# A deformable convolution on one core: one of 18 sampled columns in three of four rows made by TensorE from an image in SBUF instead of gathered

## What is computed

```
offsets = conv(x_group).reshape(B, H, W, 9, 2)
loc = clip(grid + kernel_grid + offsets, 0, 127)          # x, y
wa = (x1 - x) * (y1 - y); wb = (x1 - x) * (y - y0)
wc = (x - x0) * (y1 - y); wd = (x - x0) * (y - y0)
sampled = wa * img[y0, x0] + wb * img[y1, x0] + wc * img[y0, x1] + wd * img[y1, x1]
s = pointwise(depthwise3x3(sampled))
```

## Time and profile before

| | |
|---|---|
| timed executions | 12,372.78, 12,374.86 and 12,376.20 us, median 12,374.86 |
| span of the profiled execution, first to last instruction | 17,350.5 us |
| POOL, 9,216 gathers | busy 8,708.9 us, 945 ns each |
| DVE busy | 5,165.4 us |
| PE busy | 8,037.3 us |
| granted TensorE clock, mean | 0.694 |

### The profile page before, as it was taken

How to read it: one execution, slowest core, us unless ns; L and a number is a source line. 1 busy time by engine, 2 the same in 40 slices (tenths; PEclk the granted TensorE clock), 3 DMA queues, 4 the chain that set the end, 5 groups by cost and what they waited for, 6 DMA issues and landing times.

```text
span 17350.5 us, 102336 instructions
## 1 busy us (share of the span) xinstructions
PE 8037.3 (46%) x30934; PEld 5581.5 (32%) x30934; DVE 5165.4 (30%) x5993; ACT 1769.5 (10%) x2822; POOL 8759.5 (50%) x9300
## 2 busy tenths in 40 slices
PE   4444444445345544443335555344325555443358
PEld 2223223223234432232224443232223443222245
DVE  2222222322333233233222233223223223222323
ACT  1001101110000011100000001110000001110014
POOL 4555555455554555455554455555555444545530
PEclk7667677667667776666667777666667777666679
DMA  2222222222223321222123321222112332122233
GB/s 78 68 60 66 78 62 70 72 61 77 61 75 98 98 60 48 63 80 59 43 61 99 98 84 45 57 77 68 46 52 77 98 98 61 48 64 77 60 124 118
DMA packets 878203, 1254.74 MB, mean 72 GB/s; under 512 B 183384, under 2 KB 663064, under 8 KB 859992
## 3 DMA queue, kind: packets, MB, share of 16 engines
q0 software_dynamic: 294912, 604.57, 13.7%
q1 hardware_dynamic: 511784, 596.71, 10.7%
q10 hardware_dynamic: 71344, 51.39, 0.9%
HBM read 1069.42 MB, written 245.43 MB: 76 GB/s over the span
## 4 chain that ended last, share of the span: by engine, by line
another core or an unknown queue 40%; PE 20%; issue 19%; DVE 10%; ACT 3%; PEldq 2%; PEld 1%; SPq 1%; DMA 1%; ACTq 1%; DVEq 1%
PE acc L1307 8%; PE stage L1163 6%; DVE srow L1685 5%; PE stage L1035 2%; PEldq L483 2%; DVE gathered L1678 2%; PE pt L1294 1%; ACT stt L1008 1%; PEld acc L1307 1%; PE stage L1102 1%; PE stage L1081 1%; DMA off<-offs 1%; DVE wtn L1647 0%; SPq L694 0%
## 5 line engine op out<-in xcount | busy, mean ns | idle before, releaser
L543 POOL DMA_INDIRECT gathered<-table,idx x9216 | 8708.9, 945 | 7844.0 <-issue 4412.7
L1307 PE MATMUL acc<-stt,room 128*128 128x256 f32 (+2 forms) x15360 | 4368.5, 438 | 4763.0 <-ACT stt L1008 2491.7
L1307 PEld LDWEIGHTS acc<-stt,room 128*128 128x128 f32 (+1 forms) x15360 | 3242.4, 221 | 5803.8 <-issue 2728.6
L1685 DVE TENSOR_REDUCE srow<-gathered 128x576 f32<-128x2304 f32 x512 | 2097.1, 4096 | 324.7 <-remote 207.2
L1163 PE MATMUL stage<-room 128*128 128x128 f32 x6784 | 1035.3, 303 | 1067.5 <-issue 1049.5
L1163 PEld LDWEIGHTS stage<-room 128*128 128x128 f32 x6784 | 962.5, 218 | 1139.8 <-issue 1134.0
L1678 DVE TENSOR_TENSOR gathered<-gathered,wtb 128x2304 f32<-128x2304 f32 x512 | 1304.4, 2548 | 1.2 <-issue 1.2
L1008 ACT ACTIVATE stt<-pt 128x1024 f32<-128x1024 f32 (+1 forms) x512 | 415.6, 812 | 8375.5 <-remote 4988.2
L1666 DVE SCALAR_TENSOR_TENSOR xs<-acc,fused,xr 128x256 f32<-128x256 f32 x128 | 61.7, 482 | 3747.9 <-PE acc L1307 2206.0
L1035 PE MATMUL stage<-room,mat 128*128 128x512 f32 (+1 forms) x1360 | 776.2, 694 | 841.1 <-issue 338.9
L1294 PE MATMUL pt<-mat,srow 128*128 128x128 f32 x2048 | 427.2, 337 | 1475.6 <-DVE srow L1685 1250.7
(11 more groups left out here) (212 smaller groups left out, 4575.2 us busy)
## 6 DMA issues: line engine op xcount, KB each, us to landing
gathered<-table,idx POOLq DMA_INDIRECT x9216
room<-toep SPq DMA_DIRECT2D x48, 1792.0 KB, 7.0
room<-toep SPq DMA_DIRECT2D x64, 1280.0 KB, 8.0
room<-toep SPq DMA_DIRECT2D x64, 768.0 KB
table<-room SPq DMA_DIRECT2D x64, 512.0 KB
toep<-in_taps SPq DMA_DIRECT2D x128, 224.0 KB
gathered<-toep SPq DMA_DIRECT2D x16, 1792.0 KB, 7.0
toep<-in_taps SPq DMA_DIRECT2D x128, 160.0 KB
```

Source lines behind the costliest of these rows:

```text
L543: nc.gpsimd.indirect_dma_start(gat[r][:, k % K9 * G + k // K9, :], None, table[b].rearrange("(n e) -> n e", e=PAIR), bass.IndirectOffsetOn ...
L1307: ins = nc.tensor.matmul(sums_of[:, pairs, :], wk[0:kk, m, dx, at:at + P], stt[0:kk, slots, m, dx:dx + W], start=start and m == 0 and dx == 0,
L1685: nc.vector.tensor_reduce(srow[r % 2][:].rearrange("p (s c) -> p s c", c=CG), gat[r][:].rearrange("p s (q c) -> p s c q", q=4), AX.X, ALU. ...
```

## The change

In rows 0, 1 and 2 of each step the last column (k = 17: group 1, the tap at the lower right) is no longer gathered; POOL issues 17 indirect DMAs for these rows and 18 for row 3. The sampled values of this column are made by other engines.

Group 1's 32 channels of the whole image lie in SBUF, x on the partitions, then y, then channel (`image`, two buffers, filled by ACT's queue in one DMA for each image). Interpolation in x is a product with a matrix of "hat" weights max(0, 1 - |x - xpos|), 128 x 128 for each row (`hat_x`). PE multiplies it by the image in eight **pieces** of four channels x 128 y (`dense_piece`), alternately into the banks `acc[1]` and `pt`. DVE multiplies each piece in PSUM by hat weights in y (`hat_y`) and sums over y into four values of `srow` (`dense_column`). The hats are made once for a step (`hats`), from positions that SP's queue writes to HBM (`xrow`) and loads again to all partitions (`load_columns`); the index chain has four operations more.

```diff
+DENSE = 3
+DK = GK - 1
+PIECES = CG // 4
+        def dense_bank(j):
+            return (acc[1][:] if j % 2 == 0 else pt[:].rearrange("p a w -> p (a w)")).rearrange("p (c y) -> p c y", c=4)
...
-                        for k in range(GK):
+                        for k in range(gathered_of(r)):
                             nc.gpsimd.indirect_dma_start(
...
                         sp.wait_ge(off_used, n + 1)
                         load_offsets(n + 1, nb, ni)
+                        sp.wait_ge(hat_made, n + 1)
+                        load_columns(nb, ni)
...
+                def load_image(b):
+                    act.dma_start(image[b % 2], pixels(b)).then_inc(img_in, 16)
...
+                def dense_done(n, r):
+                    pe.wait_ge(dense_summed, PIECES * (DENSE * n + r) + PIECES + 2)
...
+                def dense_piece(n, b, r, j):
+                    pe.wait_ge(dense_summed, PIECES * (DENSE * n + r) + j + 1)
+                    nc.tensor.matmul(dense_bank(j), hat_x[:, r, :], image[b % 2][:, :, 4 * j:4 * j + 4].rearrange("x y c -> x c y"),
+                                     start=True, stop=True).then_inc(dense_p, 1)
...
                         turn_full(v, r)
-                        yield 3 * r + 3
+                        if r < DENSE:
+                            yield 3 * r + 2.1
...
+                            dense_piece(n, b, r, 0)
...
-                            products(r, slots, pairs, full[:1], start=r == 1 and not first)
+                            for j in range(6):
+                                products(r, slots, pairs, (j // 3,), start=r == 1 and not first, dxs=(j % 3,))
+                                if r < DENSE:
+                                    dense_piece(n, b, r, j + 2)
+                            if r < DENSE:
+                                yield 3 * r + 3
+                            products(r, slots, pairs, full[2:3], dxs=(0, 1))
+                            if r < DENSE:
+                                dense_done(n, r)
+                            products(r, slots, pairs, full[2:3], dxs=(2,))
                             turn_rest(r)
...
+                def hats(n):
+                    at_x = base0[:, 0, 2:3]
+                    ts(hat_x, xpos, at_x, None, ALU.subtract)
...
+                def dense_column(n, r):
+                    if r == 0:
+                        dve.wait_ge(hat_made, n + 1)
+                    for j in range(PIECES):
+                        k = PIECES * (DENSE * n + r) + j + 1
+                        dve.wait_ge(dense_p, k)
+                        at_y = hat_y[:, r:r + 1, :].to_broadcast([P, 4, H])
+                        tt(dense_bank(j), dense_bank(j), at_y, ALU.mult).then_inc(dense_weighted, 1)
+                        dve.wait_ge(dense_weighted, k)
+                        c = DK * CG + 4 * j
+                        nc.vector.tensor_reduce(srow[r % 2][:, c:c + 4], dense_bank(j), AX.X, ALU.add).then_inc(dense_summed, 1)
...
+                        if r < DENSE:
+                            yield 3 * r + 2.1
+                            dense_column(n, r)
+                        if r == ROWS - 1 and not last:
+                            hats(n + 1)
```

More of the change, by code:

```diff
@@ L298, in in_pairs @@
             return [pair + twice(*shape) for pair in first]
+        image = twice(H, CG)
+        ramp, y_far = carve(W + 1), carve(ROWS)
+        xpos, hat_y = several(2, DENSE, W)
+        hat_x = gathered[:, 0:DENSE, GK - 1, :]
+        spare = image[1].rearrange("p y c -> p (y c)")
+        cw0 = spare[:, 0:12 * C].rearrange("p (k c) -> p k c", c=C)
+        offw = spare[:, 12 * C:12 * C + 12 * NOFF].rearrange("p (k o) -> p k o", o=2 * NOFF)
         at[0] = 0
@@ L782, in _ @@
                 meet = meeting(sp)
-                for a in (*bands_out, offs_out, x2_out, *cx_out, *mix_out, *abg_out, *s_out, *res_out, *table_out):
+                for a in (*bands_out, offs_out, xrow_out, x2_out, *cx_out, *mix_out, *abg_out, *s_out, *res_out, *table_out):
                     sp.sem_inc(a, 1)
@@ L1018, in _ @@
                 act.sem_inc(right_entries, 2)
-                drive(act, meet, step, lambda: None, {"modulate": ln_and_exp, "close": ln_and_exp},
+                drive(act, meet, step, lambda: load_image(0), {"modulate": ln_and_exp, "close": ln_and_exp},
                       {"conv_norm": norm, "shift": shift, "conv_shift": lower_part, "table_norm": norm,
@@ L1299, in turn_rest, with products @@
                         .then_inc(turned, 1)
-                def products(r, slots, pairs, chunks, start=False):
+                def dense_piece(n, b, r, j):
+                    pe.wait_ge(dense_summed, PIECES * (DENSE * n + r) + j + 1)
+                    nc.tensor.matmul(dense_bank(j), hat_x[:, r, :], image[b % 2][:, :, 4 * j:4 * j + 4].rearrange("x y c -> x c y"),
+                                     start=True, stop=True).then_inc(dense_p, 1)
+                def products(r, slots, pairs, chunks, start=False, dxs=range(3)):
                     at = BLOCK_AT[r] * C
@@ L1305, in products @@
                         kk = P if m < MCH - 1 else C
-                        for dx in range(3):
+                        for dx in dxs:
                             ins = nc.tensor.matmul(sums_of[:, pairs, :], wk[0:kk, m, dx, at:at + P],
@@ L1318, in step @@
                         turn_full(v, r)
-                        yield 3 * r + 3
+                        if r < DENSE:
+                            yield 3 * r + 2.1
+                            if r == 0:
+                                if first:
+                                    pe.wait_ge(img_in, 16 * (b + 1))
+                                pe.wait_ge(hat_made, n + 1)
+                            dense_piece(n, b, r, 0)
+                        else:
+                            yield 3 * r + 3
                         pe.wait_ge(full_ready, v + 1)
@@ L1327, in step @@
                         if r == 0 and isinstance(n, int) and n == 0:
+                            for j in range(1, PIECES):
+                                dense_piece(n, b, r, j)
+                            yield 3 * r + 3
+                            dense_done(n, r)
                             turn_rest(r)
@@ L1636, in indices @@
                     then(ts(loc[:], loc[:], 0.0, float(W - 1), ALU.max, ALU.min))
+                    y_of = xy(loc, 1)[:, :, DK]
+                    then(stt_(y_far, y_of, float(W - 1), y_of, ALU.is_ge, ALU.add))
                     then(nc.vector.tensor_copy(inti, loc[:]))
@@ L1696, in first_index @@
                     indices(0)
+                    hats(0)
                 def start():
```

86 lines of the change are left out of this document (69 added, 17 removed).

## The result

The changed kernel takes **14,971.26 us** (median of 4 runs, 14,968.94 to 14,972.43); the kernel before took 12,374.35 beside it. The ratio is **1.2098 [1.2081, 1.2115]**: 21% slower. I had said 14,200, between 12,900 and 15,300. The direction, the mechanism and the price of a piece were as forecast; the forecast is 760 us short, one claim on the profile was wrong, and another is shown only in part.

What follows compares the result with a forecast made beforehand. POOL's gathers bound the kernel before, 89.9 us a step; afterwards DVE and PE in lockstep would. 128 x 90.9 = 11,635, + 1,375 + 290 + 100 + 188 + 620 gave 14,210, said as 14,200 us (+15%), range 12,900 to 15,300.

Steps and rivals of the forecast that it cites:

- price of a piece: On PE, two records reading the image at every 32nd value: 1.74 us, bounds 0.87 and 1.83.
- another is shown only in part: In the changed profile, POOL's gathers stay 1.25 us apart, but it waits for `summed` and `idx` in every step.
- 40 us of waits: Kernel before: POOL's own work sums to 12,333 us of 12,374.86, leaving some 40 us for all its waits.
- The row at 256 bytes: PE's last-image triangle products, reading `turned_a` at every 64th value: 0.220 us each against 0.113 for adjacent columns.
- The first rival: Strided reads at 128 bytes cost nothing: piece 0.87 us, POOL stays the bound, 12,235 us, faster by 1.1%; chance 7%.
- The break-even of 1.1 us a piece: The change is faster when a piece costs PE less than about 1.1 us: average step below 89.9 us.
- Pieces of a row: From the end of DVE's sum, PE's transposes, pieces and products and DVE's last multiply and sum take 18.7 us.
- The step without a flow: DVE's own 34.8 us plus three rows' pieces of 18.7 us each: 90.9 us, above POOL's 86.1.
- The flows and stage starts: Other stage work on DVE with its waits adds 1,375 us; 41 meetings of all engines add 290 us.
- the 7 us of a stage start: At each of 41 stage starts PE finishes some 9 us after DVE's last sum, DVE 2.6: 7 us uncovered.
- SP's wait for the hats: It holds only SP's loads back; positions are needed 5 us into the index chain, so normally no cost.
- The profiled span: The changed kernel's profiled span will again be longer than its timed executions; before, by 5,000 us.

Runs made afterwards that it cites:

- the second profile: The unchanged kernel before, profiled once more: a span of 12,352.8 us, 12,354.56 us timed.

## Why the prediction came out as it did

**What bounds the kernel before: right, but not its 40 us of waits.** POOL sets every step, and the kernel without pieces falls to POOL's new floor. But the 40 us that my sum left for POOL's waits are none. In the second profile POOL waits for indices and sums some 3 us in all after its first gather; its 9,215 intervals are 1.2524 us on average and not 1.248, which makes 40.6 us. The 38.3 us of waits above come near to 40 by chance: 35.3 of them lie in the 181 us that the sum has before the first gather.

**Price of a piece: right.** Forecast 1.74 us, measured 1.71. The row at 256 bytes was the proper one to lean on: from 16 bytes on the price is the same within 7%. That a strided read does not care about the clock was right too. The first rival would have had no chance even at its own price: the kernel with adjacent columns goes at a pair of 1.33 us, below the rival's 1.4, and is still slower than before (1.043), since its steps average 94.4 us where the rival had POOL's 86.1 and 315 us over in all. The break-even of 1.1 us a piece was wrong with it, for the same reason as the sum, the flows.

**Pieces of a row: right.** From the end of DVE's sum to the last piece's sum I had 18.7 us; the median over 384 rows is 18.95.

**The step without a flow: 2 us short.** Forecast 90.9; the second and third image's steps with no flow take 93, 1 us of it in the three rows' pieces and 1 in DVE's own work. Over 128 steps that is 269 us.

**The flows and stage starts: the term that was mis-sized.** I added 1,375 for flows, 290 for stage starts and 100 for images, 1,765 us. The trace of after gives 127 steps of 110.65 us on average (from line 1803's first instruction to the next step's), so 14,053 - 127 x 93 = 2,242 us, 477 more. By stage, us above 93 a step (mine, without the 7 us of a stage start; measured, with it):

| stage | steps | mine | measured |
|---|---|---|---|
| depthwise | 24 | 22 | 29.4 |
| operands | 12 | 4 | 21.1 |
| table | 12 | 7.5 | 15.6 |
| context, triangle | 12 | 7.5 | 14.3 |
| modulate | 12 | 16 | 16.5 |
| close | 12 | 11 | 12.5 |
| conv | 9 | 16.3 | 18.2 |
| normalisations | 12 | 10 | 23.5 |

With the 7 us of each stage start taken off, my sum lacks 184 us in operands, 156 in depthwise, 78 in the normalisations, 76 in table, and 39 in context and triangle; the remaining terms together were 54 us too high. In operands, depthwise and table the gap is a chain through another engine or queue that POOL's pace had hidden. Operands and table I had priced by DVE's own instructions, depthwise by PE's matmuls but not by ACT's answers behind them. Operands and table fell to 9.1 and 10.7 when the loads were left out. In depthwise DVE waits for ACT's activations between its two operations of a row (DVE's timeline of after, around such a wait):

```profile
4653.96 0.69 DVE L1625 TENSOR_REDUCE room<-room 128x4 f32<-128x512 f32 x1 [4.98 <-ACT room L943]
...
4660.28 0.69 DVE L1625 TENSOR_REDUCE room<-room 128x4 f32<-128x512 f32 x1 [4.31 <-ACT room L943]
```

In the normalisations it is the price of the meeting: in the six of the first image's steps DVE waits some 24 us at the head of the index chain, and with the loads left out still 22 us, there for PE at line 508, where I had 7.

I had written that SP's wait for the hats costs nothing "unless a large load is ahead of them". I looked at the new load of positions and not at the old one of offsets beside it, which turned from hidden to late without any edit to it. The 269, the 477 and some 15 at the start and the end make up the 761 us between the sum's 14,210 and the result. What context and triangle lack was not tried by itself, nor was why PE comes so late to those six meetings.

**The profiled span: wrong.** I said that the span after would again be longer than the timed runs; it is 14,968.5 beside 14,971.26. A stretched execution is an event, not a property of the kernel: it befell another kernel too, the one with three rows of adjacent pieces, once in four executions (17,072.34 us, the others 13,111 to 13,119). What causes it is open.

## What to carry to other kernels

Work that is moved off the bound onto idle engines is free only up to the slack of each step: with one such row of four the kernel gained 0.9%, with three it lost 21%. Look at how PE's moving operand lies in SBUF before counting its columns: a float32 operand at a stride of 16 bytes or more took twice the time here at the full clock, and the same sums from adjacent columns gave back 15 of the 21 points. When the bound moves, price every chain that the old bound hid, loads and other engines' answers too, and not only the busy time of the engine that becomes the bound; and don't add or subtract such chains one by one where they run beside each other.

## What was not expected of the hardware

At a granted clock of 1.00 PE read a float32 moving operand (the one that streams through, here the image) at every 2nd value as fast as adjacent ones (0.90 us a piece of 512 columns), at every 4th in 1.78, at every 8th in 1.82, at every 32nd in 1.71, so a stride of 16 or 32 bytes is slightly dearer than one of 128. At 0.50 an adjacent piece and one at every 32nd value took nearly the same, 1.71 and 1.73 us. DVE's read of the accumulator at 128 bytes costs nothing (691 ns against 692). And one execution of the kernel before was 5,000 us longer than the next (17,350.5 and 12,352.8 us of span), with the same median pitch of its gathers, 1.249 us.
